# The last group's queries in two halves, and the last rows in two pieces of two tiles

## The reference

```
h = layernorm(x);  q = h Wq;  latent = (h Wk + h Wv) W_down;  k = latent W_up_k;  v = latent W_up_v
scores = clip(q k^T / sqrt(128)) * exp(-0.0001 |i - j|), clipped
x = x + (softmax(scores) v) Wo
h = layernorm(x);  y = fp8(h / s_in) fp8(W8 / s_k) * s_in * s_k
x = x + bf16(y) + bias
```

## Time and profile before

| | us |
|---|---|
| median of 3 runs (lowest, highest) | 513.15 (513.13, 513.18) |
| the profiled execution | 513.14 |
| its span | 511.3 |
| ScalarE's last exponential ends | 493.94 |
| TensorE's last weighing ends | 495.42 |
| VectorE's last operation ends | 509.20 |

### The profile page before, as it was taken

One profiled execution on the slowest core, in us unless ns is written; L12 is line 12 of the kernel. 1 busy time (PEld: TensorE's weight loads), 2 busy tenths in 40 slices (PEclk: granted clock), 3 DMA queues, 4 the chain that ended last, 5 costly groups with the idle time before them and its releaser, 6 DMA issues.

```text
span 511.3 us, 9473 instructions
## 1 busy us (share of the span) xinstructions
PE 478.2 (94%) x3456; PEld 113.3 (22%) x3456; DVE 268.5 (53%) x639; ACT 486.7 (95%) x541; POOL 218.5 (43%) x285
## 2 busy tenths in 40 slices
PE   7899999999999999999999999999999999899991
PEld 3312221132122212222121221223121212122220
DVE  6514554555554564646644554544644555445536
ACT  3789999999999999999999999999999999999983
POOL 0889509883720249873450229957101031002110
PEclk9999999999999999999999999999999999999996
DMA  6589979877543326647834223568744222220000
GB/s 185 182 252 230 333 168 222 319 211 229 164 97 87 73 56 213 219 129 236 261 78 98 67 68 120 173 217 252 247 96 128 67 68 69 55 56 2 1 22 24
DMA packets 56755, 73.79 MB, mean 144 GB/s; under 512 B 6976, under 2 KB 32256, under 8 KB 56704
## 3 DMA queue, kind: packets, MB, share of 16 engines
q1 hardware_dynamic: 55616, 72.72, 49.4%
q10 hardware_dynamic: 1088, 0.41, 0.3%
HBM read 35.40 MB, written 35.65 MB: 139 GB/s over the span
## 4 chain that ended last, share of the span: by engine, by line
PE 43%; ACT 39%; issue 12%; DVE 4%; DMA 1%; ACTq 0%; DVEq 0%
ACT probs L803 38%; PE ps L1019 22%; PE ps L1003 12%; PE ps L999 2%; PE ps L913 1%; PE ps L908 1%; DVE ps L1269 1%; PE ps L880 1%; DVE pv_out L1282 1%; PE ps L876 1%; DMA wuv_s<-L_attn_W_up_v 1%; DVE mv L1316 0%; PE ps L933 0%; PE ps L870 0%; PE ps L885 0%
## 5 line engine op out<-in xcount | busy, mean ns | idle before, releaser
L803 ACT ACTIVATE probs<-ps 128x1024 f32<-128x1024 f32 x512 | 473.4, 1101 | 5.8 <-DVE ps L1269 2.6
L1019 PE MATMUL ps<-probs,V 128*9 128x512 f32 x2048 | 267.8, 595 | 0.4 <-DVE pv_out L1282 0.4
L1269 DVE TENSOR_TENSOR ps<-ps,consts 128x256 f32<-128x256 f32 (+1 forms) x256 | 140.6, 564 | 157.2 <-PE ps L1003 150.7
L1003 PE MATMUL ps<-Qs,Ks 64*128 64x512 bf16 x992 | 171.8, 384 | 13.9 <-ACT probs L803 11.8
L1003 PEld LDWEIGHTS ps<-Qs,Ks 64*128 64x128 bf16 x992 | 44.6, 93 | 283.6 <-ACT probs L803 271.8
L1282 DVE COPY pv_out<-ps 105x512 f32<-105x512 f32 x28 | 19.4, 691 | 58.0 <-PE ps L1019 58.0
L605 POOL TENSOR_SCALAR rs<-mv 128x4 f32<-128x4 f32 (+1 forms) x10 | 2.3, 228 | 99.2 <-DVEq L1456 98.5
L1019 PEld LDWEIGHTS ps<-probs,V 128*9 128x9 f32 x2048 | 30.5, 88 | 62.2 <-issue 54.3
L688 POOL TENSOR_TENSOR xs<-xs,magic 128x512 f32<-128x512 f32 x7 | 8.9, 1273 | 56.5 <-DVE magic L1335 56.5
L701 POOL TENSOR_TENSOR yb<-yb,bias_s 128x512 bf16<-128x512 bf16 x7 | 8.1, 1155 | 49.9 <-DVE yb L1407 49.5
L641 POOL TENSOR_TENSOR parts<-sq,parts 128x1024 bf16<-128x1024 f32 (+1 forms) x16 | 28.7, 1791 | 1.3
(11 more groups left out here) (152 smaller groups left out, 285.0 us busy)
## 6 DMA issues: line engine op xcount, KB each, us to landing
Qs<-qp_dram SPq DMA_DIRECT2D x58, 256.0 KB, 4.6
qp_dram<-parts SPq DMA_DIRECT2D x14, 768.0 KB, 6.3
Ks<-kp_dram SPq DMA_DIRECT2D x28, 256.0 KB, 3.9
kp_dram<-parts SPq DMA_DIRECT2D x12, 384.0 KB, 4.4
kp_dram<-parts SPq DMA_DIRECT2D x6, 768.0 KB, 5.1
Ks<-kp_dram SPq DMA_DIRECT2D x34, 128.0 KB, 2.8
qp_dram<-parts SPq DMA_DIRECT2D x7, 512.0 KB, 8.1
X<-L_attn_x SPq DMA_DIRECT2D x9, 256.0 KB, 2.9
```

The lines of the kernel that those rows point to most:

```text
L803: nc.scalar.activation(probs[:, quad % RING, 2 * jp:2 * jp + 2, :].rearrange("p j n -> p (j n)"), ps_all[:, bank * CH:(bank + 2) * CH], AC ...
L1003: last = nc.tensor.matmul(bank, Ks[half, g, jp, key_cols(v, kc)], Qs[half, g, jp, qh, v, :], start=True, stop=True)
L1019: last = nc.tensor.matmul(pv[32 * j:32 * j + VW, :], V[:, unit // 2 * NB + kc, HG * j + g, :], probs[:, quad % RING, j, :], start=i == 0, ...
L1269: nc.vector.tensor_tensor(own, own, factors, ALU.mult).then_inc(fixed, 1)
```

## The change

In the last group the eight quads are gone through twice, first for queries 0 to 255, then for queries 256 to 511. A slot is now one quad of one half: its four heads, 256 queries each, which fill the same two banks. So a slot has four score matmuls of 256 columns, one exponential of 1,024 columns, and its own weighing of four matmuls of 256 columns (`qk_half`, `weigh_half`), four slots behind the scores. The corrections of the group become four, of 512, 1,024, 1,024 and 512 elements, in place of eight. ScalarE's exponential of a slot waits for the weighing four slots before. When the first half's eight weighings are done, VectorE copies its sums; its turn stands in TensorE's queue after slot 510, its transposes back after slot 511, its projection before the last two weighings. The tail goes in two pieces of two tiles, VectorE's steps for them interleaved by hand. The banks change, and each half's rows are stored and loaded as its own block of 256 rows (1 KB runs).

```diff
+HALF = CH // 2
+LAST_GROUP = QUADS - NB
+HALF_SLOTS = 2 * LAST_GROUP
...
+def half_slot(s):
+
+    h, i = divmod(s - HALF_SLOTS, NB)
+    return h, LAST_GROUP + i
...
+        pairs = (range(0, 2), range(2, 4))
+
+        sum_banks = (7, 4)
...
-                    sp.dma_start(out[rows(LAST), :].rearrange("(p t) d -> p (t d)", p=P)[:, piece_cols[i]],
-                                 X1[:, LAST % 2, piece_cols[i]]
+                    sp.dma_start(out[rows(LAST), :].rearrange("(h p t) d -> h p (t d)", h=2, p=P)[i],
+                                 X1[:, LAST % 2, half_cols[i]]
...
+                if s >= HALF_SLOTS:
+                    act.wait_ge(pv_done, s - HALF_SLOTS + LAST_GROUP - RING + 1)
+                elif jp == 0 and quad >= RING:
...
+                if s >= HALF_SLOTS:
+                    h, quad = half_slot(s)
+                    nc.scalar.activation(probs[:, quad % RING, :, half_cols[h]].rearrange("p (u i) n -> p i u n", i=2),
+                                         ps[:, bank:bank + 2, :].rearrange("p i (u n) -> p i u n", u=2),
+                                         ACT.Exp, scale=SCALE).then_inc(exp_done, 1)
+                    continue
...
             nc.scalar.activation(unread[:, 2:3], ones[:, :], ACT.Sqrt)
+            deviation(2, mv2[:, half_tiles[0], :], rs2[:, :, half_tiles[0]])
...
+            def qk_half(s):
+                h, quad = half_slot(s)
+                unit, g, kc = place_of(quad)
+                v, qh = variant(quad)[0], unit % 2
+                for j in range(HG):
+                    rows = slice(64 * (j % 2), 64 * (j % 2) + 64)
+                    last = nc.tensor.matmul(ps[:, 2 * (s % 3) + j % 2, half_cols[j // 2]],
+                                            Ks[rows, g, j // 2, key_cols(v, kc)],
+                                            Qs[rows, g, j // 2, qh, v, half_cols[h]], start=True, stop=True)
+                last.then_inc(qk_done, 1)
+
+            def weigh_half(s):
+                h, quad = half_slot(s)
+                unit, g, kc = place_of(quad)
+                i = quad % NB
+                pe.wait_ge(exp_done, s + 1)
+                if i == 0 and h == 0:
+                    pe.wait_ge(pv_copied, quad // NB)
+                elif i == 0:
+
+                    pe.wait_ge(pv_half, 1)
+                for j in range(HG):
+                    last = nc.tensor.matmul(pv[32 * j:32 * j + VW, half_cols[h]],
+                                            V[:, unit // 2 * NB + kc, HG * j + g, :],
+                                            probs[:, quad % RING, j, half_cols[h]], start=i == 0, stop=i == NB - 1)
+                last.then_inc(pv_done, 1)
...
+            for s in range(HALF_SLOTS, SLOTS):
+                k = s - HALF_SLOTS
+                pe.wait_ge(exp_done, s - 2)
+                qk_half(s)
+                if k % 2 == 0 and LAST_GROUP + k // 2 in PE_SIDE:
+                    job(*PE_SIDE[LAST_GROUP + k // 2])
+                if k in (0, 2):
+                    weigh(LAST_GROUP - 2 + k // 2)
+                elif k >= 4:
+                    weigh_half(s - 4)
+                if k == 14:
+
+                    pe.wait_ge(y_ready, LAST)
+                    turn_group(G - 1, work, pairs[0])
+            turn_back(0, work[:, HALF:CH])
+            weigh_half(SLOTS - 4)
+            weigh_half(SLOTS - 3)
             pe.wait_ge(x1_in[LAST % 2], 16 * (LAST // 2 + 1))
...
+            pe.wait_ge(ot_halves[0][0], 1)
+            rows_of_x(0)
+            project_half(0)
+            rows_of_x(1)
+            weigh_half(SLOTS - 2)
+            weigh_half(SLOTS - 1)
+
+            pe.wait_ge(pv_half, 2)
+            turn_group(G - 1, ps[:, 5, :], pairs[1])
+            turn_back(1, ps[:, 3, 0:HALF])
+            project_half(1)
...
+            divide_rows_by_sums(G - 1, work, half_tiles[0], G)
+            dve.wait_ge(back_ps, 1)
+            nc.vector.tensor_copy(OT[:, LAST % 2, half_cols[0]], work[:, HALF:CH]).then_inc(ot_halves[0][0], 1)
...
+                half_stats(0)
+                copy_half(1)
+                divide_rows_by_sums(G - 1, ps[:, 5, :], half_tiles[1], G + 1)
+                half_rows(0)
+                half_stats(1)
+                half_power(0)
+                half_rows(1)
+                half_grid(0)
+                half_power(1)
+                half_grid(1)
+                half_result(0)
+                half_result(1)
```

More of the change, by code:

```diff
@@ L106, in variant, with to_fix @@
     return MINUS, (r * P, CH, 2 * P)
+HALF = CH // 2
[4 more added lines that the diff above has]
+    return h, LAST_GROUP + i
+def to_fix(s):
+    if s < HALF_SLOTS:
+        return variant(s // 2)[1]
+    h, quad = half_slot(s)
+    span = variant(quad)[1]
+    if span is None or span[0] // HALF != h:
+        return None
+    return span[0] - h * HALF, span[1] - h * HALF, span[2]
 FIXED = [0]
 for _s in range(SLOTS):
-    FIXED.append(FIXED[-1] + (variant(_s // 2)[1] is not None))
+    FIXED.append(FIXED[-1] + (to_fix(_s) is not None))
 FIRST_VALUES = 1
@@ L967, in job @@
                     multiply(i, work)
-            pairs = (range(0, 2), range(2, 4))
             pe.wait_ge(eye_in, 16)
@@ new lines, in rows_of_x, with project_half @@
+            def rows_of_x(half):
+                nc.tensor.matmul(ps[:, sum_banks[half], 0:HALF], eye[:, :], X1[:, LAST % 2, half_cols[half]],
+                                 start=True, stop=False)
+            def project_half(half):
+                pe.wait_ge(*ot_halves[half])
+                for t in pairs[half]:
+                    last = nc.tensor.matmul(ps[:, sum_banks[half], t % 2 * P:t % 2 * P + P],
+                                            OT[:, LAST % 2, t * P:(t + 1) * P], wo_s[:, :],
+                                            start=False, stop=t % 2 == 1)
+                last.then_inc(proj_halves[half][0], 1)
@@ L1024, in _, with turn_back @@
+            def turn_back(half, bank):
+                pe.wait_ge(turned, G + half)
+                for t in pairs[half]:
+                    last = nc.tensor.transpose(bank[:, t % 2 * P:t % 2 * P + P], o_tok[:, t, :], eye[:, :])
+                last.then_inc(back_ps, 1)
+            for quad in range(LAST_GROUP):
                 unit, g, kc = place_of(quad)
@@ L1063, in _ @@
                     second_keys()
-            weigh(QUADS - 2)
-            pe.wait_ge(x1_in[LAST % 2], 16 * (LAST // 2 + 1))
[L1067 to L1085, removed]
+            pe.wait_ge(stage_in[G - 1], 16 * STAGED * B)
@@ L1089, in last_steps @@
                     pe.wait_ge(*xq_halves[i])
[L1090 to L1094, removed]
+                    for t in pairs[i]:
+                        last = nc.tensor.transpose(ps[:, 2 * i, :].bitcast(BF16)[:, t % 2 * P:t % 2 * P + P],
                                                    xn2[:, t * P:(t + 1) * P], eye16[:, :])
@@ L1097, in last_steps @@
                     pe.wait_ge(*xqT_halves[i])
-                    for t in piece_tiles[i]:
-                        last = nc.tensor.matmul(ps[:, i, t % 3 * P:t % 3 * P + P], xqT[:, t * P:(t + 1) * P], kq[:, :],
+                    for t in pairs[i]:
+                        last = nc.tensor.matmul(ps[:, 2 * i + 1, t % 2 * P:t % 2 * P + P], xqT[:, t * P:(t + 1) * P], kq[:, :],
                                                 start=True, stop=True)
@@ L1259, in fix @@
             def fix(s):
-                quad = s // 2
-                _, span = variant(quad)
+                span = to_fix(s)
                 if span is None:
@@ L1477, in _ @@
                 b = unit // 2
+                if quad == QUADS - 2:
+                    copy_half(0)
                 fix(2 * quad)
@@ L1502, in finish, with half_stats, half_rows @@
                 empty_work("y", unit)
+            divide_rows_by_sums(G - 1, work, half_tiles[0], G)
+            dve.wait_ge(back_ps, 1)
+            nc.vector.tensor_copy(OT[:, LAST % 2, half_cols[0]], work[:, HALF:CH]).then_inc(ot_halves[0][0], 1)
             def last_unit():
                 own = X1[:, LAST % 2, :]
[L1507 to L1518, removed]
+                sums = [ps[:, sum_banks[t // 2], t % 2 * P:t % 2 * P + P] for t in range(4)]
+                def half_stats(half):
                     dve.wait_ge(*proj_halves[half])
-                    for t in range(2 * half, 2 * half + 2):
+                    for t in pairs[half]:
                         step(nc.vector.bn_stats(stats2[:, t, :], sums[t]))
[L1522 to L1525, removed]
-                    for t in tiles:
+                    settle()
+                    for t in pairs[half]:
+                        step(nc.vector.bn_aggr(mv2[:, t, :], stats2[:, t, :]))
+                    settle()
+                    dve.sem_inc(var_ready, 1)
+                def half_rows(half):
+                    tiles = half_tiles[half]
+                    invert_deviation(2 + half, mv2[:, tiles, :], rs2[:, :, tiles])
+                    for t in pairs[half]:
```

89 lines of the change are left out of this document (48 added, 41 removed).

## The result

The changed kernel takes 515.52 us in the median of four runs (514.98 to 515.77), the kernel before 513.15. The ratio is 1.0044, with a 95% interval of 1.0032 to 1.0057, so it is slower by 2.4 us. It lies in the range of 512.2 to 516.0 and on the side that was given the largest chance, but it is twice as far from the kernel before as the forecast's 1.15 us, and above the forecast's own spread of 513.7 to 515.2. The profiled execution is the fastest of the four, 514.98, with a span of 513.2. A profile is of one execution, so the same point of a kernel can lie some 0.1 us earlier or later in another profile; where less than that matters, the text counts from a nearby row.

A forecast was written before the change was run, and what follows sets the result against it. TensorE's queue was taken to set the last group's end, then a chain led by VectorE: +3.3 for the stream, -2.3 in the tail, +0.15 for the store, +1.15 in all, so 514.3 us; range 512.2 to 516.0.

The forecast's parts named there:

- the side that was given the largest chance: Whole kernel: slower than before, above 514.2 us, chance 0.48.
- TensorE's queue: Last group's stream: TensorE has no slack and sets the end; last weighing ends at 498.75, 3.3 us later.
- the forecast's fourth rival: Last group's stream: halves cost exactly stream and fixed part or half, so it cancels; 513.0 to 513.9, chance 0.20.
- The new wait for y: TensorE before the first half's turn: stands 1.0 us until VectorE copies the former unit's product, behind slot 510's correction.
- Exposed weights: Half score products: two further weight loads not hidden, 0.10 per slot, +1.1 us, 515.4; chance 0.12.
- dear matmuls: Half weighings: each costs its upper bound, 0.66 us; +1.4 to 1.7, 515.9; chance 0.08.
- Drains that hide: Changes between scores and weighings: fixed 0.10 to 0.13 vanishes for halves; last weighing at 496.8, 512.4 us; chance 0.18.
- VectorE from the last weighing on: Tail after the last weighing: VectorE's queue is the bound; 11.4 us against 13.7, 2.3 saved.
- Copy, turn and division of the second half: First tail step after the last weighing: takes 1.4 us again, as for the first half before.
- The clock: TensorE's last four steps: still follow idle time, so no gain counted; at 2.4 GHz it would be 0.3 less.
- The store: Last store at the kernel's end: 128 KB instead of 64, between 1.6 and 1.9 us, so +0.15.
- a sign of being wrong: Tail: not near 11.4 us, because ScalarE's steps come later than VectorE asks for them.

The follow-up runs named there:

- the run of 515.78: The changed kernel timed once more with nothing altered: its profiled execution took 515.78 us, the median 515.55, ratio 1.0060.
- its own repair: Kernel before with only the second half's rows of x moved behind the last weighing on TensorE: 512.83 us, ratio 0.9991.
- the kernel with the 17 matmuls: Changed kernel with VectorE's branch early and product copied first, plus TensorE's branch turned round and 17 unread matmuls in its idle time: 513.31 us.

## Why the prediction was right, and where it was not

- *TensorE's queue.* Right, with the unit prices a little high: half weighing 0.55 (taken 0.57), score product 0.32 (0.33). The last weighing ended at 498.26; forecast 498.75. The sum with the lower prices, those of the forecast's fourth rival, gives 498.3. Too wide was the sentence that "what it is given to do counts in full", with the last exponential "long done": it was done 0.43 us before the last weighing started, and taking 0.53 us of work away gained 0.3.
- *The new wait for y.* Right: a stand of 1.0 us before the first half's turn, and 0.95 us came back when the copy went ahead of slot 510's correction.
- *Exposed weights and dear matmuls.* Fallen: a slot of four score matmuls takes 0.32, as one of two did. The rule of the Trainium skill, "TensorE: Matmul & The Clock Gate", section "The mechanism", that a weight load hides only behind another row group would ask for more; the row shows none of it. The same section also lets a load go ahead into a background weight buffer, and with that the row agrees; the prediction had left this half out. *Drains that hide* fell too, since the fixed 0.1 stays with each half.
- *VectorE from the last weighing on.* Here the prediction failed, in its cause: "Copy, turn and division of the second half ... so 1.4 again". It took 2.8 (498.26 to 501.05). The step took the copy as free to start with the last weighing, as it had in the kernel before, and did not see the branch that the change had moved work in front of: before, VectorE's 4.55 us of idle time ahead of this copy covered it. From the division on the sum was near: 7.3 where 7.44 was forecast, and 2.6 where 2.55 was. So the tail is 12.7 and not 11.4, which the prediction had named as a sign of being wrong, though for another reason (late steps of ScalarE).
- *The clock.* "The clock gives back nothing I count" missed that it can also take. For the last four steps nothing changed. But in the run of 515.78 the clock falls before the transposes back and the projection, at a cost of 0.77 us, and that is the difference between this run and the profiled 514.98. That the other runs near 515.5 are of this kind is argued from their lower mean clock (0.988 against 0.990), as none of them has a profile.
- *The store* took 2.2 us to the end of the span as before (2.15): less than 0.1 more, not 0.15.

So the profiled 514.98, 1.84 above 513.14, is 0.6 that the forecast had right (its 1.15 with the true prices and store), 1.4 of exposed branch, and 0.1 less in the steps behind it. The 0.5 to 0.8 more of the other three runs is put down to the clock, as one profile shows it. With the branch entered early or taken out the kernel takes 513.65 and 513.75, against 513.8 that the forecast gives with those prices. That 515.52 lies in the stated range at all is luck: the range reached above 515.2 only for exposed weights and dear matmuls, and neither came.

The change as such is no gain; it needs two repairs in VectorE's queue even to draw level. With the branch early, the product first and the rows of x late it has the lowest median here, 512.37; the kernel before with its own repair is at 512.83.

## What to carry to other kernels

Before moving work forward past a runtime branch, look for the idle time that covered the branch: "issue" after a branch is a jump, and it costs whoever has become early. Put the jump where its engine has some 4 us to spare (here it took 3.1 to 3.8), and count the one at the end of a path that falls through. When work is put in front of a wait in an in-order queue, ask what else stands between that wait's releaser and its turn: here one copy and one correction exchanged were worth 1 us.

## What the runs showed that I had not expected

A jump to the path behind the general one leaves VectorE idle for 3.06 to 3.49 us, the reading of the flag included, in the seven profiles that show it. On TensorE the record of the branch alone is 3.34 us in the changed kernel and 3.78 in the kernel with the 17 matmuls, and 0.09 where it falls through. On VectorE the branch's own record is 0.07 us even where it jumps, and the loss stands behind it as idle time that names nobody. TensorE's clock fell within 500 to 501 in one execution and 503 to 504 in another of the same kernel, with the same idle times before, and a pair of transposes after the fall cost 0.25 us more, a projection 0.5.
